# Feed-forward block of a fused two-layer kernel: where the step-size chain, its transposes and the parameter store stand

## The reference

```
# feed-forward of layer 1: int4 weights with group scales, I = 1792, group of 128 inputs
gate_score   = silu(x @ Wg.T);  intermediate = gate_score * (x @ Wu.T)
g            = silu(intermediate @ Wd.T)            # Wg, Wu, Wd = q * scale per group
# step sizes of the state-space mixer, 128 heads, chunks of 128 tokens
dt    = softplus(h @ w_dt.T + dt_bias);  A = -exp(A_log)
A_cs  = cumsum(A * dt, within a chunk)
decay = exp(A_cs[last] - A_cs);  last-decay of a chunk = exp(A_cs[last])
```

## Time and profile before

| what | us |
|---|---|
| median of 3 runs | 2070.99 (2067.04 to 2071.72) |
| the profiled execution, its own time | 2064.4 |
| its span in the trace | 2062.6 |
| gate/up phase of layer 1, m = 1 to 13, in the trace | about 241 to 400 |
| its down phase | about 402 to 455 |
| mixer | 458 to the end |

### The profile page before, as it was taken

How to read it: one execution, slowest core, us unless ns; L and a number is a source line. 1 busy time by engine, 2 the same in 40 slices (tenths; PEclk the granted TensorE clock), 3 DMA queues, 4 the chain that set the end, 5 groups by cost and what they waited for, 6 DMA issues and landing times.

```text
span 2062.6 us, 32803 instructions
## 1 busy us (share of the span) xinstructions
PE 1970.5 (96%) x10886; PEld 1583.5 (77%) x10886; DVE 1598.5 (78%) x2985; ACT 1477.8 (72%) x2964; POOL 1226.1 (59%) x848
## 2 busy tenths in 40 slices
PE   7997888889999999999999999999999999999986
PEld 6563666667788888888888888888888888888865
DVE  7767787856778787787778777878787878878776
ACT  5234765535778787787778787878787877878774
POOL 5653665643566665666566665566656666666655
PEclk9998999999999999999999999999999999999998
DMA  5513323343333333334343433333433334243333
GB/s 201 189 57 124 96 93 107 98 148 111 120 117 113 116 114 104 128 96 135 104 128 95 130 123 115 116 104 117 128 114 107 114 114 128 90 130 114 128 111 115
DMA packets 114328, 242.00 MB, mean 117 GB/s; under 512 B 23665, under 2 KB 24689, under 8 KB 113522
## 3 DMA queue, kind: packets, MB, share of 16 engines
q1 hardware_dynamic: 110322, 227.32, 34.2%
q0 software_dynamic: 3840, 12.59, 2.0%
HBM read 227.01 MB, written 12.85 MB: 116 GB/s over the span
## 4 chain that ended last, share of the span: by engine, by line
PE 74%; DVE 1%; issue 1%; ACT 1%; DMA 0%; SPq 0%; DVEq 0%; ACTq 0%
PE s_ps L71 13%; PE s_ps L73 13%; PE s_ps L72 13%; PE s_ps L1778 6%; PE s_ps_o L73 6%; PE s_ps_o L71 6%; PE s_ps_o L72 6%; PE s_ps L1748 5%; PE s_ps L1786 4%; PE s_ps L1740 3%; PE s_ps L1768 1%; PE s_ps L1726 1%; ACT s_lm L1858 0%; DMA s_wo_raw<-in_w_out 0%; PE s_ps L1732 0%
## 5 line engine op out<-in xcount | busy, mean ns | idle before, releaser
L2160 POOL TENSOR_TENSOR w_lo<-w_raw,w_hi 128x1024 fp32r<-128x1024 f32 x142 | 340.0, 2400 | 549.7 <-ACT w_hi L1840 549.7
L71 PE MATMUL s_ps<-h_hi,w_hi 128*128 128x512 f32 x1152 | 464.0, 403 | 10.1 <-DVE s_hid L2009 6.1
L73 PE MATMUL s_ps<-h_hi,w_lo 128*128 128x512 f32 x1152 | 451.4, 392 | 0.0
L72 PE MATMUL s_ps<-h_lo,w_hi 128*128 128x512 f32 x1152 | 449.5, 390 | 0.0
L2004 DVE SCALAR_TENSOR_TENSOR s_cv<-s_ps,s_par,s_cv 128x511 f32<-128x511 f32 (+2 forms) x480 | 355.9, 744 | 18.5 <-ACT s_cv L1883 12.6
L2177 POOL TENSOR_TENSOR s_lm<-s_lm,s_cbt 128x512 f32<-128x512 f32 x256 | 326.2, 1296 | 12.5 <-ACT s_lm L1865 12.5
L1858 ACT ACTIVATE s_lm<-s_rows,s_steps 128x128 f32<-128x128 f32 x1024 | 312.5, 391 | 2.2 <-PE s_ps L1778 2.2
L1883 ACT ACTIVATE s_cv<-s_ps,s_par 128x512 f32<-128x512 f32 x160 | 124.4, 778 | 227.5 <-PE s_ps L73 227.5
L71 PEld LDWEIGHTS s_ps<-h_hi,w_hi 128*128 128x128 f32 x1152 | 217.2, 189 | 56.3 <-DVE s_hid L2009 6.9
L73 PEld LDWEIGHTS s_ps<-h_hi,w_lo 128*128 128x128 f32 x1152 | 216.9, 188 | 47.6
L72 PEld LDWEIGHTS s_ps<-h_lo,w_hi 128*128 128x128 f32 x1152 | 217.7, 189 | 41.4
(11 more groups left out here) (279 smaller groups left out, 4121.4 us busy)
## 6 DMA issues: line engine op xcount, KB each, us to landing
w_raw<-in_w_in SPq DMA_DIRECT2D x144, 512.0 KB, 3.6
s_rows<-acs_dram SPq DMA_DIRECT2D x256, 256.0 KB, 4.4
s_wo_raw<-in_w_out SPq DMA_DIRECT2D x128, 256.0 KB, 3.2
w_raw<-in_gu_q SPq DMA_DIRECT2D x14, 512.0 KB, 3.7
f_d_q<-in_d_q SPq DMA_DIRECT2D x28, 256.0 KB, 2.6
f_d_w<-in_d_s SPq DMA_DIRECT2D x28, 256.0 KB, 3.4
table<-shifted SPq DMA_DIRECT2D x16, 256.0 KB, 2.6
xs<-in_x SPq DMA_DIRECT2D x8, 256.0 KB, 6.2
```

The costliest lines, as they stand in the source:

```text
L71: nc.tensor.matmul(dst, l_hi, r_hi, start=start, stop=False)
L72: nc.tensor.matmul(dst, l_hi, r_lo, start=False, stop=False)
L73: return nc.tensor.matmul(dst, l_lo, r_hi, start=False, stop=stop)
L2160: nc.gpsimd.tensor_tensor(w_lo[:, slot, :], w_raw[:, slot, :], w_hi[:, slot, :].bitcast(F32), ALU.subtract).then_inc(w_lo_ready, 1)
```

## The change

The lengths of the loops and the arithmetic stay. What moves:

- `dve_rest` goes to m = 2 and 3, one half each; `dve_dt` keeps its first two instructions at m = 4 and 5, and the rest becomes `dve_sums` at m = 6 and 7.
- `act_decay` goes to the down phase, i = 18 and 19, `dve_decay` to i = 19 and 20; the transposes go behind the down steps i = 20 (`TURN_AT`) and 21, into the banks 4 to 7, which hold nothing any more once `act_out` has read half 0; the copies follow at i = 21 and 22 on DVE and on ACT. Step m = 8 becomes a step like the others.
- SP stores `acs` at m = 10 and `m_group` after the last load of down weights.
- At the seam: `act_silu(13, 1)` goes to i = 15, `dve_inner(13, 1)` to i = 16, POOL's `add_sums(13, 1)` behind `rest_down(14)`; DVE does `dve_in_lo(13)` between the two rounds of its last groups.
- In the down phase DVE does `dve_in_lo(i)` ahead of `dve_scale_down(i + 1)`.
- ACT splits the mixer's first weights at i = 26 and 27, POOL after its last `rest_down`.
- The last down step signals each of its four tiles (through `dt_proj`, which is free by then), and `act_out` of half 1 waits for its own tile.

```diff
-TURN_STEP = 8
+TURN_AT = KI + 6
...
-            if t == TB - 1:
+            if i == 2 * KI - 1:
+                mm.then_inc(dt_proj, 1)
+            elif t == TB - 1:
                 mm.then_inc(down_done, 1)
...
-            act.wait_ge(down_done, KI * (j // TB + 1))
+            if j < TB:
+                act.wait_ge(down_done, KI)
+            else:
+                act.wait_ge(dt_proj, NB + j - TB + 1)
...
             dve.tensor_tensor(dt[:, c], rest[:, n, :], u1[:, n, :], ALU.add).then_inc(dt_ready, 1)
+
+        def dve_sums(link, n):
+
+            dve, c = nc.vector, slice(n * SEQ, (n + 1) * SEQ)
+            step = e[:, n, :]
             dve.wait_ge(dt_ready, n + 1)
             dve.wait_ge(aexp_ready, 1)
...
-        def dve_groups(dve, m, n):
+        def dve_groups(dve, m, n, rounds=(2, 3)):
...
                 load_gate_up(m)
                 load_down(m)
-                if m == TURN_STEP:
+                if m == KI - 4:
                     sp.wait_ge(acs_ready, NT)
                     sp.dma_start(acs_dram, acs[:]).then_inc(stored, 16)
-                if m == TURN_STEP + 2:
-                    sp.wait_ge(group_ready, 2)
-                    sp.wait_ge(group_by_act, 2)
-                    sp.dma_start(group_dram, group[:]).then_inc(stored, 16)
...
+            sp.wait_ge(group_ready, 2)
+            sp.wait_ge(group_by_act, 2)
+            sp.dma_start(group_dram, group[:]).then_inc(stored, 16)
             for j in range(TB, NT):
                 g_store(sp, j)
             sp.wait_ge(stored, 32)
...
             for m in range(1, KI):
-                if m == TURN_STEP:
-                    pe.wait_ge(group_added, 4 * half_at(m, 0))
...
-                    continue
                 pe_gate_up(pe, m, m - 1)
             for i in range(KI - 1, 2 * KI):
                 pe_down(pe, i)
+                if i == TURN_AT:
+                    pe.wait_ge(g_ready, TB)
+                    pe.wait_ge(dt_ready, NB)
+                    pe_turn(dt, 4)
+                    pe.wait_ge(acs_ready, NT)
+                    pe_turn(acs, 6)
+                if i == TURN_AT + 1:
+                    pe.wait_ge(dd_ready, 3 * NB)
+                    pe.wait_ge(group_ready, 1)
+                    pe_turn(decay, 4)
+                    pe.wait_ge(group_by_act, 1)
+                    mm = nc.tensor.matmul(ps[:, 6, :], ones[:], diag[:].rearrange("p c h -> p (c h)"),
+                                          start=True, stop=True)
+                    mm.then_inc(turned, 1)
...
-                if m == TURN_STEP - 2:
-                    act_decay(act, 0)
-                    act_decay(act, 1)
-            act_silu(act, KI - 1, 1)
             for i in range(KI, 2 * KI):
                 act_down(act, i)
                 act_in(act, i)
+                if i == KI + 1:
+                    act_silu(act, KI - 1, 1)
                 if i < KI + TB:
                     act_out(act, i - KI)
-                c = i - KI - TB
+                if i == KI + TB:
+                    act_decay(act, 0)
+                if i == KI + TB + 1:
+                    act_decay(act, 1)
+                if i == TURN_AT + 1:
+                    act_copy_group(act)
+                if i == TURN_AT + 2:
+                    act_copy_last(act)
+                c = i - 2 * KI + 2
                 if 0 <= c < 2:
...
-                if m == 3:
-                    dve_rest(0)
-                    dve_rest(1)
+                if m in (2, 3):
+                    dve_rest(m - 2)
                 if m in (4, 5):
                     dve_dt(link, m - 4)
-                if m == TURN_STEP - 1:
-                    dve_decay(0)
-                    dve_decay(1)
+                if m in (6, 7):
+                    dve_sums(link, m - 6)
                 dve_inner(dve, m, 0)
-                dve_groups(dve, m, 1)
-                dve_in_lo(dve, m)
-            dve_inner(dve, KI - 1, 1)
+                if m < KI - 1:
+                    dve_groups(dve, m, 1)
+                    dve_in_lo(dve, m)
+            dve_groups(dve, KI - 1, 1, (2,))
+            dve_in_lo(dve, KI - 1)
+            dve_groups(dve, KI - 1, 1, (3,))
             for i in range(KI, 2 * KI):
+                dve_in_lo(dve, i)
                 if i + 1 < 2 * KI:
                     dve_scale_down(dve, i + 1)
-                dve_in_lo(dve, i)
+                if i == KI + 2:
+                    dve_inner(dve, KI - 1, 1)
+                if i in (TURN_AT - 1, TURN_AT):
+                    dve_decay(i - TURN_AT + 1)
+                if i in (TURN_AT + 1, TURN_AT + 2):
+                    dve_group(dve, i - TURN_AT - 1)
...
-            add_sums(KI - 1, 1)
             for i in range(KI, 2 * KI):
                 rest_down(i)
...
+                if i == KI:
+                    add_sums(KI - 1, 1)
+            for c in range(2):
+                pool.wait_ge(weights.hi_ready, c + 1)
```

More of the change, by code:

```diff
@@ L1037, in dve_dt @@
             dve, c = nc.vector, slice(n * SEQ, (n + 1) * SEQ)
-            step = e[:, n, :]
             dve.wait_ge(rest_ready, n + 1)
@@ L1064, in group_part, with dve_group, act_copy_last @@
             return group[:, :, i * NT * HG:(i + 1) * NT * HG].rearrange("p g (t h) -> p t g h", t=NT)
-        def dve_group(dve):
-            dve.wait_ge(turned, 1)
-            nc.vector.tensor_copy(group_part(0), group_banks(0)).then_inc(group_ready, 1)
-            dve.wait_ge(turned, 3)
-            nc.vector.tensor_copy(group_part(1), group_banks(0)).then_inc(group_ready, 1)
+        def dve_group(dve, i):
+            dve.wait_ge(turned, 2 * i + 1)
+            nc.vector.tensor_copy(group_part(i), group_banks(4)).then_inc(group_ready, 1)
         def act_copy_group(act):
             act.wait_ge(turned, 2)
-            nc.scalar.activation(group_part(2), group_banks(2), ACT.Copy).then_inc(group_by_act, 1)
+            nc.scalar.activation(group_part(2), group_banks(6), ACT.Copy).then_inc(group_by_act, 1)
+        def act_copy_last(act):
             act.wait_ge(turned, 4)
             nc.scalar.activation(group[:, :, 3 * NT * HG:].rearrange("p g (c h) -> p c g h", c=4),
-                                 ps[:, 2, :].rearrange("p (c g h) -> p c g h", c=4, g=GROUPS),
+                                 ps[:, 6, :].rearrange("p (c g h) -> p c g h", c=4, g=GROUPS),
                                  ACT.Copy).then_inc(group_by_act, 1)
@@ L1083, in dve_in_lo @@
                                     in_hi[:, i % 2, :].bitcast(F32), ALU.subtract).then_inc(in_lo_ready, 1)
-        def dve_groups(dve, m, n):
+        def dve_groups(dve, m, n, rounds=(2, 3)):
             h = half_at(m, n)
-            for k in (2, 3):
+            for k in rounds:
                 for part in range(2):
@@ L1206, in _ @@
             for m in range(1, KI):
-                if m == TURN_STEP:
-                    pe.wait_ge(group_added, 4 * half_at(m, 0))
-                    pe.wait_ge(dt_ready, NB)
-                    pe_turn(dt, 0)
-                    pe.wait_ge(acs_ready, NT)
-                    pe_turn(acs, 2)
-                    for t in (0, 1):
-                        pe_down_tile(pe, m - 1, t)
-                    pe.wait_ge(dd_ready, 3 * NB)
-                    pe.wait_ge(group_ready, 1)
-                    pe_turn(decay, 0)
-                    pe.wait_ge(group_by_act, 1)
-                    mm = nc.tensor.matmul(ps[:, 2, :], ones[:], diag[:].rearrange("p c h -> p (c h)"),
-                                          start=True, stop=True)
-                    mm.then_inc(turned, 1)
-                    for t in (2, 3):
-                        pe_down_tile(pe, m - 1, t)
-                    pe.wait_ge(group_ready, 2)
-                    pe.wait_ge(group_by_act, 2)
-                    pe.wait_ge(gu_f_ready, m + 1)
-                    for n in range(NB):
-                        for k in range(KD):
-                            pe_group(pe, m, n, k)
-                    continue
                 pe_gate_up(pe, m, m - 1)
@@ L1262, in _ @@
             for m in range(KI):
-                if m == TURN_STEP:
-                    act_copy_group(act)
                 if m:
@@ L1328, in _ @@
             for m in range(KI):
-                if m == TURN_STEP:
-                    dve_group(dve)
                 dve_groups(dve, m, 0)
```

7 lines of the change are left out of this document (2 added, 5 removed).

## The result

| | before | after |
|---|---|---|
| median, five runs each | 2067.04 (2061.45 to 2071.72) | **2048.81** (2045.87 to 2053.97) |
| profiled execution, its own time | 2064.4 | 2045.87 |
| its span in the trace | 2062.6 | 2044.1 |

The change makes the kernel faster: the ratio of the times is 0.9913 (interval 0.9888 to 0.9938), a saving of 2067.04 - 2048.81 = 18.2 us. The forecast was 2056.3 and a saving of 14.7. Of the 7.5 us between forecast and median, 4.0 are the base: the forecast was taken off the median of the first three runs (2070.99), and with five runs the kernel before stands at 2067.04. The other 3.5 are the saving.

The account below looks back on a forecast made before the run. PE and DVE were taken as both nearly full in each gate/up step. Savings of 14.5 there and 1.8 in the tail, less 1.6 lost in the down phase, gave 14.7 off 2070.99: 2056.3 us, range 2049.5 to 2063.5.

Parts of the forecast that it names:

- m = 1 to 4: Gate/up steps: most of the 3.6 us excess stays, half the difference was absorbed before; 0.8 us saved.
- The turn, m = 5 and m = 6: Gate/up steps: 9.0 us saved at the turn (m = 8), 3.7 at m = 5, 1.0 at m = 6.
- The seam: Start of the down phase: `down(14)` follows at once, and a 1.9 us wait ahead of `down(15)` replaces the one removed.
- DVE's new order: Down loop: scaling behind `in_lo` lengthens each step to 3.18 us against 2.92, PE waiting 0.4 us in each.
- rival A: Down phase: the loop does not lengthen, giving 3.1 us more and up to 5 from hidden DVE work; about 2052, chance 0.20.
- the walk: Down phase reckoned step by step in times of the earlier trace: end at 456.1 against 454.5, 1.6 us lost.
- The turn in the down phase: d_hi(20) to d_hi(23): PE's 4.4 us come on top of the matmuls; 13.9 us against 9.5 for three loops, 4.3 lost.
- The tail: From PE's end to the mixer: start falls from 4.0 to 2.2 us after PE's end; 1.8 saved (0.5 to 2.2).
- The stores: Down phase: `m_group` issued 9.5 us before PE's end lands in 6.6 us, hidden; `acs` at m = 10 waits for nothing.
- B: Down phase: turn and seam cost more, waits of 2 us or more bringing PE's lower level; about 2063, chance 0.17.
- C: Down phase: waits of 0.4 us per loop keep PE at its lower level, 31 us slower; 2087, chance 0.04.
- D: Gate/up steps m = 5 to 8: long for another reason than the chain, half stays; sum within 4 us, chance 0.04.

Follow-up runs that it names:

- b2: Kernel after with chain gathered, old DVE down order, old seam, old weight-split places and one-piece tail, leaving the turn's move: stage 207.9 us against 199.2.
- a1: Kernel after with the step-size chain gathered again at m = 3 to 5: m = 1 to 7 take 86.2 us, 3.3 more.
- b1: Kernel after with the silu, product, `in_lo` and POOL sums of the seam back ahead of the down loop: down phase 59.1 us, 0.6 more.
- a2: Kernel after with DVE's scaling of i + 1 ahead of `dve_in_lo(i)` from i = 15 on: down phase 58.4 us, 0.2 less.
- c2: Kernel after with half 0's silus paired at i = 16 and 17, POOL's sums spread, later g stores, and scaling first from i = 17: down 56.7 us.
- a4: Kernel after with the silus of half 1 waiting for all four tiles: tail 3.1 us, 1.2 more; down phase 59.6, 1.0 more.

## Why the prediction was right, and where it was short

Two terms of the sum had the wrong size, what DVE's idle time absorbs and what the transposes cost, and the base was 4.0 us too high. Where time is saved and where it is lost came out as forecast.

*What bounds the kernel: right, but read one level too coarse.* "Both nearly full, so that a microsecond added to DVE's order in a step is nearly a microsecond on the step" held. The working then took half of DVE's idle time as absorbing, in every step, for what was added and for what was removed. The step that failed is "half the difference was absorbed before: 0.8 saved", for m = 1 to 4: 2.3 were saved. The gap is 1.25 us long and stands in one place; the first instructions put there fill it, and the ones behind them pay in full. The part that is now `dve_sums(0)` stood last in m = 4, behind a full gap, so taking its 1.8 us out made the step 1.9 shorter. The half of `dve_rest` that went from m = 3 saved 0.6, and in m = 2 it cost 0.2. One row of the timeline of an undisturbed step would have shown it.

*The turn, m = 5 and m = 6: right in number, with luck in it.* 9.1 for 9.0, 3.7 for 3.7, 1.2 for 1.0. The 1.3 us taken for an added `dve_sums` turned out as 1.5 (12.39 against 10.91), but out of two errors that cancel: it takes 2.85 us in m = 6, as its scaling takes 1.53 and not "at most 0.7", and the gap absorbs 1.25 and not 0.6. And the 4.6 us by which m = 5 was too long were put down to the chain, where up to 1.8 stand with the lower clock. b2 shows 14.0 us for the move of the turn, a1 and b2 2.3 to 3.3 for the spread.

*The seam: right to 0.2 us.* `down(13)` was forecast 5.8 us after the scaling of m = 13 (5.78), `down(14)` at once, 1.9 us of wait ahead of `down(15)` (2.07). b1 shows that a wait did take the place of the one removed.

*DVE's new order: right in mechanism.* The loop was forecast at 3.18 and measured 3.18 to 3.20 (with 0.2 us of wait in it, not 0.4), with the very hand-over named: scaling behind `in_lo`, ACT behind the scaling. By this rival A falls. It gave about 2052 and so came nearer to the measured 2048.8 than the forecast did, but its loop of 2.92 is in no profile of the kernel after. What the walk did not see is what the order buys: a2 and c2 put it back and met the loads, which were hidden by it.

*The turn in the down phase: the second step that failed.* It was priced at 4.3 us, and `down(20)` to `down(23)` took 12.47, 2.9 over three loops. The term that was mis-sized is "PE's 4.4 us come on top". Its larger part, 3.1 us for sixteen transposes, measured 415.74 - 414.07 = 1.67; the other, 1.3, measured 419.91 - 418.58 = 1.33. The row taken for the price stood where PE had its lower level. Windows of both kernels show it, the kernel before first (columns as above):

```profile
324.00:328.00 4.00, 2.30 (x12) 2.31 (x13) 2.77 (x5) 0.19 (x1) 3.74 (x3) 0.75 0.33 106
328.00:330.00 2.00, 2.00 (x10) 1.81 (x9) 0.69 (x1) 0.83 (x1) 1.58 (x2) 0.65 0.18 50
```

```profile
413.00:416.00 3.00, 3.00 (x23) 2.74 (x22) 2.85 (x3) 0.00 (x0) 0.84 (x1) 1.00 0.45 165
```

A granted clock of 1.00 is the 2.4 GHz level, 0.65 and 0.75 a stretch that is in part at 1.2. The working of the down phase spoke of the clock, but took a price from such a stretch for a place where nothing makes PE wait long. b2 has the transposes at 1.03 and 1.04 us as well.

*`act_decay`, `dve_decay`, `dve_inner`:* 0.6 + 0.6 forecast, 0.64 + 0.1 measured (steps of 3.83 and 3.30 at 404.10 and 407.93, against 3.19). DVE's slack of 1.2 us a loop covered its part almost wholly.

*The tail: 2.1 for 1.8, in part by luck.* The signals are worth 1.2 (a4); the other 0.9 is the issuing of the g stores, which the sum did not have. POOL's split is what ends last, 1.4 us after PE (forecast 1.5); the table load came 3.6 us before PE's end and so cost nothing.

*The stores: right.* Issued 11 us ahead (9.5 forecast), landed in 8.6 instead of the 6.6 of the earlier trace rows, still 2.4 before PE's end.

Together: 2.1 us in the gate/up phase (14.5 forecast, 16.6 measured), 1.3 in the down phase and 0.3 in the tail make the 3.7 by which the saving in the stage was too small. B is out in its size, as the down phase is shorter than forecast; its mechanism is real, since in a2 and a4 the wait ahead of `down(15)` did bring the lower clock, at about 1.0 us in a4. C is refuted by the clock of 1.00 in steps with a wait of 0.2 us each. D is refuted in the main by the steps of m = 5 to 7, which came free; but it had a point in m = 5, with the clock that the base profile was granted there.

## What to carry to other kernels

In an order written out by hand, find the gap of the engine in one step of the timeline: in this kernel what was moved into it was free up to its length and paid in full beyond it, and a mean of idle time over the window said neither. A price taken from a row is only good at the clock that the row stood in, so look at the granted clock of those few microseconds before an instruction's time is carried to another place. And what a reordering costs in its ring may be what keeps loads ahead of their use: test it both with the old seam and with the new.
